# Degree stage of a two-layer graph network: the weighting of the one-hots moves from GpSimd to ScalarE, and the tile counts leave PSUM once for four groups

## What is computed

```python
# layer 0: a graph convolution with self loops; row = src, col = dst, w = edge_weight (1 for the loops)
deg = segment_sum(w, row, N)
dinv = where(deg > 0, deg ** -0.5, 0)
agg = segment_sum((dinv[row] * w * dinv[col])[:, None] * x[col], row, N)
x = layernorm(x + agg @ W.T + b)
# layer 1: messages by an MLP over (x[src], x[dst], attr), summed at dst, then a gated update
m = relu(concat(x[src], x[dst], attr) @ W1.T + b1) @ W2.T + b2
aggr = zeros.at[dst].add(m)
x = layernorm(x + gru(aggr, x))
```

## Time and profile before

| | us |
|---|---|
| Time, median of 3 runs | 11367.97 |
| Lowest and highest run | 11355.69, 11370.47 |
| Span of the profiled execution, first to last instruction | 11347.2 |
| `counts`, from its first one-hot to the last f32 product's end | 149.9 to 1479.6 |

### The profile page before, as it was taken

The page is one execution under the profiler, slowest core; times in us unless marked ns, Lnnn a source line. Parts: engine busy times, 40 slices in busy tenths (PEclk is TensorE's granted clock), DMA queues, the critical chain, the costliest instruction groups (busy, mean ns, idle before and its releaser), DMA issues. The chain is left out here.

```text
span 11347.2 us, 232069 instructions
## 1 busy us (share of the span) xinstructions
PE 7401.2 (65%) x59805; PEld 5933.9 (52%) x59806; DVE 5957.9 (53%) x18225; ACT 2279.0 (20%) x7946; POOL 7635.7 (67%) x7653
## 2 busy tenths in 40 slices
PE   4777733333333333333366665999999999999999
PEld 3666621111122222222255554888888888888885
DVE  6999953333333333333499985444444444444443
ACT  1000001111111111111277751111111111111111
POOL 3666637777777777777755531777777777777771
PEclk9999965555555555555555555555555555555555
DMA  6500022222222222222244432333333333333321
GB/s 246 235 0 0 0 50 78 77 77 79 77 77 77 77 77 77 77 77 77 75 110 111 110 94 79 89 86 86 86 86 86 86 85 86 86 86 86 86 82 34
DMA packets 627617, 950.45 MB, mean 84 GB/s; under 512 B 202831, under 2 KB 381213, under 8 KB 627329
## 3 DMA queue, kind: packets, MB, share of 16 engines
q1 hardware_dynamic: 427582, 640.84, 19.8%
q0 software_dynamic: 200000, 309.20, 9.6%
HBM read 690.33 MB, written 259.09 MB: 84 GB/s over the span
## 5 line engine op out<-in xcount | busy, mean ns | idle before, releaser
L1251 POOL DMA_INDIRECT tables<-a_half,src_i x3125 | 3069.1, 982 | 1271.1 <-issue 945.2
L853 POOL DMA_INDIRECT moved<-tables,place x3125 | 3067.7, 982 | 1083.8 <-issue 934.9
L815 PE MATMUL ps_rows<-tables,dst_hot 128*128 x10830 | 808.2, 240 | 2625.0 <-ACT tables L844 1513.1
L815 PEld LDWEIGHTS ps_rows<-tables,dst_hot 128*128 128x128 bf16 x10830 | 668.9, 125 | 2968.9 <-issue 2926.4
L1372 PE MATMUL ps_msum<-tables,src_cols 128*128 128x64 f32 x6250 | 1498.0, 427 | 0.0
L1372 PEld LDWEIGHTS ps_msum<-tables,src_cols 128*128 128x128 f32 x6250 | 1380.5, 329 | 136.6 <-issue 136.6
L1276 DVE TENSOR_TENSOR src_cols<-ps_pre,tables 128x640 f32<-128x640 f32 x625 | 515.1, 824 | 1736.3 <-DMA tables<-a_half,src_i 1732.6
L843 ACT ACTIVATE tables<-ps_rows,edge_cols 128x64 f32<-128x64 f32 x3125 | 707.3, 318 | 3357.0 <-DMA moved<-tables,place 3220.5
L779 DVE CAST place<-place_f 128x5 int32<-128x5 f32 x625 | 109.9, 176 | 2110.4 <-DMA moved<-tables,place 2107.0
L564 POOL TENSOR_TENSOR tables<-hi_hot,edge_cols 128x490 f32<-128x490 bf16 x625 | 853.6, 1366 | 472.3 <-DVE hi_hot L573 472.3
L1353 ACT ACTIVATE src_cols<-src_cols 128x640 f32<-128x640 f32 x625 | 460.5, 737 | 3511.0 <-DVE src_cols L1276 3447.0
(11 more groups left out here) (229 smaller groups left out, 10100.8 us busy)
## 6 DMA issues: line engine op xcount, KB each, us to landing
dst_rows<-in_dst SPq DMA_DIRECT2D x625, 320.0 KB
tables<-moved SPq DMA_DIRECT2D x723, 162.5 KB, 2.2
moved<-sums SPq DMA_DIRECT2D x180, 650.0 KB, 9.0
m_dst_rows<-in_dst SPq DMA_DIRECT2D x625, 160.0 KB
moved<-tables,place POOLq DMA_INDIRECT x3125
tables<-a_half,src_i POOLq DMA_INDIRECT x3125
b_rows<-b_half SPq DMA_DIRECT2D x625, 48.0 KB
base_rows<-tile_bases SPq DMA_DIRECT2D x625, 2.9 KB
```

The costliest lines, as they stand in the source:

```text
L815: last = pe.matmul(ps_rows[:, h, j * D:(j + 1) * D], dst_hot[:, slot, j * P:(j + 1) * P], cols(parts, win * (3 * D) + i * D, D), start=beg ...
L853: pool.indirect_dma_start(out=moved[:, :], out_offset=bass.IndirectOffsetOnAxis(ap=place[:, s, j:j + 1], axis=0), in_=rows[:, s, j, :], in ...
L1251: pool.indirect_dma_start(out=a_rows[:, s, j, :], out_offset=None, in_=a_dram[:, :], in_offset=bass.IndirectOffsetOnAxis(ap=src_i[:, s, j: ...
```

## The change

- The weighting of `hi_hot` leaves POOL. ACT does it instead, with five `ACT.Copy` activations of 128 x 98 per group, one for each tile, whose scale is the tile's column of weights (a pointer to one value per partition). The semaphores `hot_made` and `used` that POOL waited for are now waited for by ACT.
- The copy of the counts out of PSUM is made once for four groups (98 x 20) and not for each (98 x 5). PE fills one of the two banks over four groups, and waits for `evacuated` only at the first group of the four. ACT makes the copy after its weighting of the fourth group, when `counted` shows that PE has counted it. The last group has a copy of its own.
- The turns on ACT and PE are eight groups long, not four.
- PE waits once, at the start, for the cleared padding (`pad_cleared`).
- DVE's instructions are not changed.

```diff
+    REST = NG // S * S
...
-            pool.memset(hi_weight[:, :, :, NW:], 0.0)
-
-            def body(g, s, use, _):
-                pool.wait_ge(hot_made, g + 1)
-
-                wait(pool, used, g - (S - 1))
-                pool.tensor_tensor(hi_weight[:, s, :, 0:NW], hi_hot[:, s, :, :],
-                                   cols(weight, g * G, G).unsqueeze(2).to_broadcast([P, G, NW]), ALU.mult).then_inc(weighted, 1)
-            over_groups(pool, NG, body)
+            pool.memset(hi_weight[:, :, :, NW:], 0.0).then_inc(pad_cleared, 1)
...
         @block.scalar
         def _(act):
-            def body(g, s, use, _):
-                act.wait_ge(counted, g + 1)
-                act.activation(cols(by_window, g * G, G), ps_tile[0:NW, s % 2, 0:G], ACT.Copy).then_inc(evacuated, 1)
-            over_groups(act, NG, body)
+            def weigh(g, s):
+                act.wait_ge(hot_made, g + 1)
+
+                wait(act, used, g - (S - 1))
+                for j in range(G):
+                    last = act.activation(hi_weight[:, s, j, 0:NW], hi_hot[:, s, j, :], ACT.Copy, scale=cols(weight, g * G + j, 1))
+                last.then_inc(weighted, 1)
+
+            def body(g, t, use, _):
+                weigh(g, t % S)
+                if t % S == S - 1:
+                    act.wait_ge(counted, g + 1)
+                    act.activation(cols(by_window, (g - (S - 1)) * G, S * G), ps_tile[0:NW, t // S, 0:S * G], ACT.Copy).then_inc(evacuated, 1)
+            over_groups(act, NG, body, slots=2 * S)
+            act.wait_ge(counted, NG)
+            act.activation(cols(by_window, REST * G, (NG - REST) * G), ps_tile[0:NW, REST // S % 2, 0:(NG - REST) * G], ACT.Copy).then_inc(evacuated, 1)
             act.wait_ge(guarded, 1)
             act.activation(root[:, :], safe[:, :], ACT.Sqrt).then_inc(rooted, 1)
 
         @block.tensor
         def _(pe):
-            def body(g, s, use, _):
+            pe.wait_ge(pad_cleared, 1)
+
+            def body(g, t, use, _):
                 first, last_one = is_first(g), isinstance(g, int) and g == NG - 1
+                s = t % S
                 pe.wait_ge(hot_made, g + 1)
-
-                wait(pe, evacuated, g - 1)
+                if s == 0:
+
+                    wait(pe, evacuated, use * 2 + t // S - 1)
                 for j in range(G):
-                    last = pe.matmul(ps_tile[0:NW, s % 2, j:j + 1], hi_hot[:, s, j, :], ones_bf[:, 0:1], start=True, stop=True)
+                    last = pe.matmul(ps_tile[0:NW, t // S, s * G + j:s * G + j + 1], hi_hot[:, s, j, :], ones_bf[:, 0:1], start=True, stop=True)
                 last.then_inc(counted, 1)
...
-            over_groups(pe, NG, body)
-            pe.wait_ge(evacuated, NG)
+            over_groups(pe, NG, body, slots=2 * S)
+            pe.wait_ge(evacuated, REST // S + 1)
```

More of the change, by code:

```diff
@@ L519, in counts @@
         q_out = sb("q_out", [P, QP], I32)
-        zeroed, zero_done = sem("zeros_made"), sem("zero_done")
+        zeroed, zero_done, pad_cleared = sem("zeros_made"), sem("zero_done"), sem("weight_pad_cleared")
         hot_made, weighted, used = sem("hot_made"), sem("hot_weighted"), sem("hot_used")
```

## The result

| | before | after |
|---|---|---|
| Median of 4 runs, us | 11367.38 | 11035.03 |
| Lowest and highest, us | 11355.69, 11370.47 | 11028.62, 11050.67 |
| Span of the profiled execution, us | 11347.2 | 11026.6 |

The ratio is 0.971, with a 95% interval of 0.9696 to 0.9724. The kernel is 332 us faster; 365 us had been forecast, and the time lies in the range. The profiled execution took 11028.62 us, 2.0 us over its span.

What follows compares the result with a forecast made beforehand. In `counts`, DVE's first one-hot and POOL's multiply, excluding one another, were taken to set 2.124 us a group. 624 x (2.124 - 1.535) = 368 us gained, 3 us lost, gave 11003 us, range 10925 to 11110 us.

Steps and rivals of the forecast that it cites:

- What bounds the kernel: In `counts`, DVE's first one-hot stands still until POOL's multiply is through; without POOL's reading it falls to 0.66 us.
- The ring: In `counts` before the change, first one-hot and POOL multiply wait for each other: 0.53 + 0.25 + 1.35 = 2.13 us a group.
- Rival B: In `counts`, the first one-hot on DVE stays at 1.46 us for a reason other than POOL: 11368 us, chance 2%.
- PE is the next limit, at 1.41 us: In `counts` after the change, PE's unchanged work is a floor of 1.41 us per group at full clock.
- The price of a scaled copy: ACT's five scaled copies per group in `counts` were taken at 0.275 us each, 1.375 us together, just under PE's 1.41.
- Rival A: ACT's copies in `counts` don't overlap, or each group's wait costs ACT more: 11075 to 11247 us, chance 13%.
- the 0.38 us each: Skill-page estimate for ACT's scaled copies in `counts`, end to end: 1.91 us a group, about 11240 us.
- The new wait, once in four groups: In `counts`, ACT waits for PE's counts before weighting on, so PE stalls 0.50 us in every four groups.
- until the next copy can follow: Term of PE's stall in `counts`: 0.09 us from ACT's copy of the counts to its next scaled copy.
- Start, padding and clock: At the start of `counts`, the padding wait costs 0.2 us and low-clock f32 trains in some three groups lose 3 us.
- rival C: The PE clock falls in `counts`, 2.55 us a group; with all groups low 268 us slower, 11636 us; chance 2%.
- Rival D: In `counts`, the wait for the counts costs nothing, or copies are nearer 0.203 us: 10925 to 10956 us, chance 13%.

Runs made afterwards that it cites:

- multiply aside: Changed kernel plus a POOL multiply of the old form per group, from constants into a spare place, that nobody waits for: 11359.76 us, 1.0004 of before.
- memset: Changed kernel plus a POOL memset of 128 x 490 f32 zeros per group, which reads nothing: 11033.48 us, 0.9718 of before.
- late copy: Changed kernel, but ACT copies the counts of four groups after weighting the first group of the next four: 10899.47 us, 0.9608 of before.

## Why the prediction was right, and where its sizes were off

*What bounds the kernel.* Right, and shown. The multiply aside brings back 2.124 us a group without any data through POOL; the memset does not. DVE's full row in the profile of before held 0.8 us of standing still in each first one-hot. The ring's sum of 2.13 us was right, but its 1.35 us for the multiply was not the multiply's own time: some 0.5 us of it pass before L575 is through, so the ring holds both one-hots. Rival B (DVE isn't freed) falls with the 670 ns of L566.

*PE is the next limit, at 1.41 us.* Right: the late copy runs at 1.412 us with PE never idle.

*The price of a scaled copy.* Right: 0.268 us apart and 362 ns each, against 0.275 taken and 0.232 at the other end. The neighbour with its source in SBUF was the better guide. (At 0.232 us the forecast's own terms give a stall of 0.31 us and not 0.28; nothing rests on it.) Rival A, that the copies don't overlap, falls; the 0.38 us each, an estimate from the budget in the Trainium skill's "ScalarE: Activation LUTs", "Rules for kernel authors", are near the duration of one copy, but not near the distance between two.

*The new wait, once in four groups.* Right in place and kind, too small in size: this is the term behind the missing 33 us. The step was forecast at 0.50 us of lost PE time. In the timeline of after, the stalled step is 2.03 us or 2.28 us long against 1.41, so 0.62 and 0.87 us in turn, 0.745 on average. The term that was mis-sized is the 0.09 us "until the next copy can follow" the copy of the counts. Its measured values are 0.25 us (1140.33 to 1140.58), and 0.50 us where ACT's loop goes back. The other terms of the stall came out within 0.04 us. With 0.745 the sum gives (4 x 1.41 + 0.745) / 4 = 1.596 us a group, against 1.592 measured and 1.535 forecast; 0.057 us in 624 steps are 36 us.

These rows of the changed kernel show the distance in the first turn, which is written out, and in the loop where it goes back:

```profile
159.26 0.19 ACT L640 ACTIVATE tables<-ps_tile_counts 98x20 f32<-98x20 f32 x1 [2.80 <-PE ps_tile_counts L659]
159.34 5.44 ACT L633 ACTIVATE tables<-hi_hot,edge_cols 128x98 f32<-128x98 bf16 x20
...
1133.83 0.19 ACT L640 ACTIVATE tables<-ps_tile_counts 98x20 f32 x1 [0.56 <-PE ps_tile_counts L659]
1134.33 5.45 ACT L633 ACTIVATE tables<-hi_hot,edge_cols 128x98 f32<-128x98 bf16 x20 [0.31 <-issue]
```

In the written-out first turn, without the loop's register instructions, the distance is 0.07 to 0.09 us after waits of 0.23 to 4.92 us, in this kernel, the late copy, the copy for each group, the memset aside and sixteen groups a turn, wherever the group behind the copy is written out too. In the loop it depends on the counts. Where they had ended 0.29 us and more before the copy, as half of them had in the kernel with a copy for each group, it is 0.05 to 0.07 us. Where the copy follows their end by 0.12 to 0.15 us, it is 0.23 to 0.27 us, in the late copy too, though ACT shows no idle time there. It takes both, counts that come only just in time and the loop, and the forecast priced neither. That the way back costs the extra 0.25 us is shown by the longer turn, and once more by the last copy of the changed kernel's loop: there the loop is left and does not go back, and the distance is 0.22 us. That the other 0.16 us are the loop's register instructions, which find no queued work to hide them when ACT was held for the counts, is argued from the written-out turns; no run took those instructions out of the loop.

*Start, padding and clock.* The first f32 train starts at 153.10 us. Two trains of the start are longer, 2.25 and 1.65 us against 1.20, so about 1.5 us lost and not 3. The forecast put these longer trains down to the low clock, but the granted clock is 1.00 from 150 to 160 us in both kernels, so no row shows that, and their cause stays open. The price of rival C was read from the same trains, so no row of `counts` shows it either. The granted clock stayed at 1.00 in the whole stage, and rival C did not come about; the mean granted clock of the profiled execution falls from 0.566 to 0.553, only because the one stage at full clock is shorter.

*Rival D*, a wait that costs nothing, is not what this kernel does, but it is what the late copy makes of it: 1.412 us a group, 0.961 of before. It is the version to use, and beats both kernels.

## What to carry to other kernels

When an engine's row is full, compare the same instruction where its neighbour is idle: a duration that doubles beside GpSimd arithmetic can be a wait inside the instruction, as it was here, and then moving the GpSimd work frees more than GpSimd. When a producer is also given a periodic job that waits for its consumer, place that wait one unit of production later, so that the producer always has finished work in hand; here this one move was worth 115 us, a third of the change's own gain. And price what follows a wait in a hardware loop by itself: here it was 0.25 us, and 0.50 where the loop went back, against 0.08 in written-out code.

## What was not expected of the hardware

The distance from a ScalarE copy that waits for TensorE to the next ScalarE instruction depends on the code around it and on how late the data come. In a hardware loop it was 0.06 us where the data had been there for 0.3 us and more, 0.23 to 0.27 us where they came 0.12 to 0.15 us before the copy, and 0.50 us where the loop also went back (0.57 to 0.61 in the kernels with a copy for each group and with sixteen groups a turn). Written-out code shows 0.07 to 0.09 us even after a wait. The exclusion between VectorE and GpSimd worked both ways in every group: a multiply that GpSimd began beside the second one-hot ended 0.86 to 0.88 us after it, whatever its own length, and the first one-hot ended 0.51 to 0.54 us after the multiply. And two engines that wait for each other once per group settled into a wait in about every second group: 1.754 us a group, and not the 2.03 us that a full wait in each would give.
